# A six-layer mixture-of-experts and attention kernel on one core: expert gates from TensorE, two weight loads from ScalarE, and a transposed output projection

## The reference, cut to what matters

```python
x = x + 0.5 * _L0_ffn_ref(_layernorm(x), Wr, br, W1, b1, W2, b2)    # MOE0_A
x = x + _L0_attn_ref(_layernorm(x), wq, bq, wk, bk, wv, bv, wo, bo) # ATT0
x = x + 0.5 * _L0_ffn_ref(_layernorm(x), Wr, br, W1, b1, W2, b2)    # MOE0_B
x = x + 0.5 * _L1_ffn_ref(_layernorm(x), gate_w, expert_w, expert_b)  # MOE1_A
x = x + _L1_attn_ref(_layernorm(x), Wq, Wk, Wv, Wo)                 # ATT1
x = x + 0.5 * _L1_ffn_ref(_layernorm(x), gate_w, expert_w, expert_b)  # MOE1_B
```

```python
h = gelu(einsum('td,edh->teh', xt, W1) + b1)
o = einsum('teh,eho->teo', h, W2) + b2
y = einsum('teo,te->to', o, comb)
```

```python
V = Q * KV[:, None, :] * Z
out = V @ wo + bo
return gelu(out, approximate=True)
```

## Time and profile before

| | us |
|---|---|
| Median of 3 runs | 703.26 |
| Lowest and highest | 699.38, 709.02 |
| The profiled execution | 708.19 |
| Its span in the profile | 706.2 |
| TensorE busy in the span | 655.9 (93%) |
| VectorE, ScalarE, GpSimd busy | 465.5, 432.3, 181.3 |

### The profile page before, as it was taken

One profiled execution on the slowest core, in us unless ns is written; L12 is line 12 of the kernel. 1 busy time (PEld: TensorE's weight loads), 2 busy tenths in 40 slices (PEclk: granted clock), 3 DMA queues, 4 the chain that ended last, 5 costly groups with the idle time before them and its releaser, 6 DMA issues.

```text
span 706.2 us, 7645 instructions
## 1 busy us (share of the span) xinstructions
PE 655.9 (93%) x2395; PEld 415.2 (59%) x2395; DVE 465.5 (66%) x1059; ACT 432.3 (61%) x922; POOL 181.3 (26%) x132
## 2 busy tenths in 40 slices
PE   3699998999999999999999999999999989889974
PEld 2456565556656555676576666666566645556552
DVE  5677467643447964737769957858886757386752
ACT  4345456444447554697486478657379524968685
POOL 3120000100002111144042025214014432676565
PEclk9899999999999999999999999989999998989998
DMA  8782621063333107612223222200613000000000
GB/s 244 162 164 67 112 63 38 22 122 65 102 75 60 59 3 132 96 26 65 42 61 62 65 55 60 60 1 11 111 60 61 0 1 0 1 15 1 16 16 15
DMA packets 27026, 42.22 MB, mean 60 GB/s; under 512 B 1689, under 2 KB 8938, under 8 KB 26986
## 3 DMA queue, kind: packets, MB, share of 16 engines
q1 hardware_dynamic: 26986, 41.74, 27.1%
HBM read 40.42 MB, written 1.31 MB: 59 GB/s over the span
## 4 chain that ended last, share of the span: by engine, by line
PE 67%; ACT 12%; DVE 9%; SPq 5%; DMA 4%; issue 2%; POOL 1%; POOLq 0%; ACTq 0%; DVEq 0%
PE py L1122 26%; PE ph L900 7%; PE ph L902 7%; PE ph L901 7%; ACT stage L547 5%; ACT bc L547 4%; DMA bc<-comb_rows 3%; PE ps L1030 2%; SPq L358 2%; DVE stage L756 2%; PE ps L1031 2%; PE ps L1032 2%; SPq L331 1%; PE ps L1004 1%; PE ps L1005 1%
## 5 line engine op out<-in xcount | busy, mean ns | idle before, releaser
L596 ACT ACTIVATE g<-ph,b1col 128x512 f32<-128x512 f32 x256 | 172.7, 695 | 153.3 <-PE ph L902 120.1
L1122 PE MATMUL py<-hw,w2s 128*128 128x512 f32 x512 | 250.0, 612 | 1.9 <-DVE hw L859 1.9
L859 DVE TENSOR_TENSOR hw<-g,bc 128x1024 f32<-128x1024 f32 x128 | 166.8, 1310 | 110.4 <-ACT g L596 93.2
L1122 PEld LDWEIGHTS py<-hw,w2s 128*128 128x128 f32 x512 | 97.2, 194 | 77.7 <-issue 64.4
L900 PE MATMUL ph<-xbh,w1h 128*128 128x512 f32 x256 | 137.4, 537 | 0.0
L388 POOL TENSOR_TENSOR rstd<-vare,mhalf 128x4 f32<-128x4 f32 x24 | 35.4, 1477 | 358.3 <-DVE vare L672 358.1
L547 ACT ACTIVATE stage<-ps,comb 128x128 f32<-128x128 f32 x384 | 106.3, 564 | 10.4 <-PE ps L1032 10.2
L902 PE MATMUL ph<-xbh,w1l 128*128 128x512 f32 x256 | 102.7, 401 | 0.0
L901 PE MATMUL ph<-xbl,w1h 128*128 128x512 f32 x256 | 102.6, 401 | 0.0
L448 POOL TENSOR_TENSOR stage<-stage 128x1024 f32<-128x1024 f32 x24 | 57.4, 2393 | 68.4 <-ACT stage L547 68.4
L900 PEld LDWEIGHTS ph<-xbh,w1h 128*128 128x128 f32 x256 | 49.7, 194 | 30.8 <-issue 22.6
(11 more groups left out here) (199 smaller groups left out, 865.0 us busy)
## 6 DMA issues: line engine op xcount, KB each, us to landing
bc<-comb_rows SPq DMA_DIRECT2D x31, 1024.0 KB, 8.8
stage<-in_L_ffn_W_dram SPq DMA_DIRECT2D x4, 512.0 KB, 6.5
X<-in_L_attn_x_dram SPq DMA_DIRECT2D x4, 256.0 KB, 3.1
bc<-comb_rows SPq DMA_DIRECT2D x4, 256.0 KB, 5.5
out_dram<-X SPq DMA_DIRECT2D x4, 256.0 KB, 2.3
comb_rows<-combT SPq DMA_DIRECT2D x8, 32.0 KB, 5.3
side<-in_L_attn_wq_dram SPq DMA_DIRECT2D x1, 64.0 KB
side<-in_L_attn_wk_dram SPq DMA_DIRECT2D x1, 64.0 KB
```

The source lines that it names most:

```text
L596: nc.scalar.activation(g[:, s % 2, h, 0:w], ph[:, (HC * s + h) % RING_PH, 0:w], ACT.Gelu, bias=b1col[:, HC * e + h:HC * e + h + 1]).then_i ...
L859: V.tensor_tensor(hw[:, s % RING_HW, :, 0:w], g[:, s % 2, :, 0:w], bc[:, s // GQ % 2, s % GQ, 0:w].unsqueeze(1).to_broadcast([P, HC, w]), ...
L1122: ins = T.matmul(py[:, 0:cols], w2s[:, w], hw[:, s2 % RING_HW, h, 0:cols], start=e2 == 0 and h == 0, stop=False)
```

## The change

Four parts.

1. **Gates of the first three experts from TensorE.** `PE_GATES` is 3. After `combT` is there, TensorE multiplies it by a column of the identity spread over 128 columns, which gives the row of one expert on all partitions, in one bank of `ps` for each expert. VectorE reads the gates of slots 0 to 2 from there. SyncE reads back only the fourth expert's row for the first group.
2. **Two large loads issued by ScalarE.** W2 is issued after ScalarE's first part of W1 (L484 of the changed kernel), the expert weights of the second kind in its step `wt` (L513), which waits for all parts of `w1_ready`. The attention's and the other small loads stay with SyncE.
3. **Output projection of the first attention.** `wos` is now the stationary operand and all 512 tokens stream past it in one matmul; the result is features by tokens, so the bias is one value for each partition and goes into ScalarE's gelu. TensorE then transposes four tiles into `ps`, and VectorE adds from PSUM. On TensorE the step has one more turn. The bias matmuls and `bos` are gone.
4. **The table of turns** is another one for every engine but SyncE; its first rows show the form:

```diff
-    "PE": ("h5 l3 m2 l m3 l3 m3 l m3 l m2 h m l2 m3 h3 m l h m19 l h2 m5 l m2 h2 m7 h m5 l m2 l2 m2 l m9 l m32 l m4 l m2 h2 m2 l "
+    "PE": ("h4 l3 m4 l m h l m2 l2 m3 l m l m l2 m h m l3 m l3 h3 m h m2 h2 m15 l m4 l m2 h2 m6 h m h m4 l m2 l2 m2 l m11 l m32 l m4 "
```

The rest of the diff:

```diff
@@ -64,6 +64,7 @@
     LAG = 2
+    PE_GATES = 3
@@ -89,9 +90,8 @@
         wr0 = sb("wr0", [P, 2 * E], f32r)
         wr1 = sb("wr1", [P, 2 * E], f32r)
         qkv0h, qkv0l = sb("qkv0h", [P, 3 * P], f32r), sb("qkv0l", [P, 3 * P], f32r)
-        bqkv = sb("bqkv", [P, 3])
+        bqkv = sb("bqkv", [P, 4])
         wos = sb("wos", [P, D])
-        bos = sb("bos", [1, D])
         qkv1h, qkv1l = sb("qkv1h", [P, 3 * P], f32r), sb("qkv1l", [P, 3 * P], f32r)
         woT = sb("woT", [P, P])
         weh, wel = sb("weh", [P, E * D], f32r), sb("wel", [P, E * D], f32r)
@@ -196,12 +196,13 @@
         y_out = sem("y_out")
         comb_row = sem("comb_row")
         bc_in = [sem("bc_in0"), sem("bc_in1")]
-        bc_first = [sem(f"bc_first{e}") for e in range(GQ)]
+        gate_ps = sem("gate_ps")
+        bc_first = sem("bc_first")
 
         light = {n: sem(n) for n in ("stat", "rstd", "xn", "xt_ps", "xh", "xl", "res", "lg_ps", "shift", "expd",
                                   "comb", "ct_ps", "ct", "yt_ps")}
         a0 = {n: sem("a0_" + n) for n in ("q_ps", "k_ps", "v_ps", "relq", "relk", "v", "minq", "mink", "expq", "expk",
-                                          "vz", "o_ps", "o", "x")}
+                                          "vz", "o_ps", "o", "ot_ps", "x")}
         f1 = {(l, late): {n: sem(f"f{l}_{late}_{n}") for n in ("y_ps", "relu_a", "relu_v", "half", "quarter", "sum", "red")}
               for l in (MOE1_A, MOE1_B) for late in (0, 1)}
         a1 = {late: {n: sem(f"a1_{late}_{n}") for n in ("qk_ps", "v_ps", "relu", "v", "exp", "qk", "x", "kv", "kvh", "kvl",
@@ -327,13 +328,12 @@
                 sp.dma_start(stage[:, w1_part(i)].rearrange("p (e h) -> p e h", h=H), W1[e].rearrange("e d h -> d e h")).then_inc(w1_in[i], 16)
                 if i == 0:
                     sp.dma_start(b1row[:, :], b1.rearrange("e (c p) -> (e c) p", p=P)).then_inc(w_in["b1"], 16)
-            sp.dma_start(w2s[:, :].rearrange("p (e c o) -> p e c o", e=E, c=HC), W2.rearrange("e (c p) o -> p e c o", p=P)).then_inc(w_in["w2"], 16)
             sp.dma_start(b2s[:, :], b2).then_inc(w_in["w2"], 16)
             for i, (w, b) in enumerate(((wq, bq), (wk, bk), (wv, bv))):
                 sp.dma_start(stage2[:, E + P * i:E + P * (i + 1)], w).then_inc(w_in["small"], 16)
                 sp.dma_start(bqkv[:, i:i + 1], b.rearrange("(p a) -> p a", a=1)).then_inc(w_in["small"], 16)
             sp.dma_start(wos[:, :], wo).then_inc(w_in["small"], 16)
-            sp.dma_start(bos[:, :], bo.rearrange("(a p) -> a p", a=1)).then_inc(w_in["small"], 16)
+            sp.dma_start(bqkv[:, 3:4], bo.rearrange("(p a) -> p a", a=1)).then_inc(w_in["small"], 16)
             for c in range(1, NCH):
                 sp.dma_start(X[:, col(c)].rearrange("p (t d) -> p t d", d=D), x_t[:, tiles(c), :]).then_inc(x_in[c], 16)
 
@@ -347,13 +347,11 @@
                     if k >= 2:
                         sp.wait_ge(hw_ready, GQ * (k - 1))
                     if k == 0:
-                        for e in range(GQ):
-                            sp.dma_start(bc[:, 0, e:e + 1, 0:wide(c)], comb_dram[l // 2, e:e + 1, col(c)].partition_broadcast(P)).then_inc(bc_first[e], 16)
+                        sp.dma_start(bc[:, 0, PE_GATES:GQ, 0:wide(c)], comb_dram[l // 2, PE_GATES:GQ, col(c)].partition_broadcast(P)).then_inc(bc_first, 16)
                         continue
                     sp.dma_start(bc[:, k % 2, :, 0:wide(c)], comb_dram[l // 2, q * GQ:(q + 1) * GQ, col(c)].partition_broadcast(P)).then_inc(bc_in[k % 2], 16)
                     if k == 1:
                         sp.wait_ge(w1_ready, W1_PARTS)
-                        sp.dma_start(stage[:, 0:E * D].rearrange("p (e h) -> p e h", e=E), expert_w.rearrange("e d h -> d e h")).then_inc(w_in["we"], 16)
                         for i, w in enumerate((Wq, Wk, Wv, Wo)):
                             sp.dma_start(stage[:, E * D + P * i:E * D + P * (i + 1)], w).then_inc(w_in["l1"], 16)
                         sp.dma_start(stage[0:E, E * D + 4 * P:E * D + 5 * P], gate_w).then_inc(w_in["l1"], 16)
@@ -482,6 +480,8 @@
                 for i in range(W1_PARTS):
                     act.wait_ge(w1_in[i], 16)
                     nc.scalar.activation(w1h[:, w1_part(i)], stage[:, w1_part(i)], ACT.Copy).then_inc(w1_high, 1)
+                    if i == 0:
+                        act.dma_start(w2s[:, :].rearrange("p (e c o) -> p e c o", e=E, c=HC), W2.rearrange("e (c p) o -> p e c o", p=P)).then_inc(w_in["w2"], 16)
                     yield
 
             def q0(l, c):
@@ -509,6 +509,8 @@
                 yield
 
             def wt(l, c):
+                act.wait_ge(w1_ready, W1_PARTS)
+                act.dma_start(stage[:, 0:E * D].rearrange("p (e h) -> p e h", e=E), expert_w.rearrange("e d h -> d e h")).then_inc(w_in["we"], 16)
                 for _ in range(WROUNDS + 1):
                     yield
 
@@ -525,7 +527,7 @@
                     nc.scalar.activation(t_m[:, i, :], t_m[:, i, :], ACT.Exp).then_inc(a0["exp" + n], 1)
                 yield
                 act.wait_ge(a0["o_ps"], c + 1)
-                nc.scalar.activation(osb, ps[:, 1, :], ACT.Gelu_apprx_tanh).then_inc(a0["o"], 1)
+                nc.scalar.activation(osb, ps[:, 1, :], ACT.Gelu_apprx_tanh, bias=bqkv[:, 3:4]).then_inc(a0["o"], 1)
                 yield
 
             def f1_(l, c):
@@ -759,8 +761,8 @@
                     ins = V.scalar_tensor_tensor(vv[:, q], t_m[:, 0, q], kvs[:, 1, s:s + 1], t_r[:, 0, q], ALU.mult, ALU.mult)
                 ins.then_inc(a0["vz"], 1)
                 yield
-                dve.wait_ge(a0["o"], c + 1)
-                V.tensor_tensor(X[:, col(c)], X[:, col(c)], osb, ALU.add).then_inc(a0["x"], 1)
+                dve.wait_ge(a0["ot_ps"], c + 1)
+                V.tensor_tensor(X[:, col(c)], ps[:, 2, :], X[:, col(c)], ALU.add).then_inc(a0["x"], 1)
                 yield
 
             def f1_(l, c):
@@ -849,15 +851,17 @@
             def main(s, half):
                 if half and s < SLOTS:
                     dve.wait_ge(g_ready, HC * (s + 1))
-                    if s < GQ:
-                        dve.wait_ge(bc_first[s], 16)
+                    if s < PE_GATES:
+                        dve.wait_ge(gate_ps, s + 1)
+                    elif s == PE_GATES:
+                        dve.wait_ge(bc_first, 16)
                     elif s % GQ == 0:
                         dve.wait_ge(bc_in[s // GQ % 2], 16 * ((s // GQ + 1) // 2))
                     if s >= RING_HW:
                         dve.wait_ge(slot_done, s - RING_HW + 1)
                     w = wide(MAIN[s // E][1])
-                    V.tensor_tensor(hw[:, s % RING_HW, :, 0:w], g[:, s % 2, :, 0:w],
-                                    bc[:, s // GQ % 2, s % GQ, 0:w].unsqueeze(1).to_broadcast([P, HC, w]), ALU.mult).then_inc(hw_ready, 1)
+                    gates = ps[:, s, 0:w] if s < PE_GATES else bc[:, s // GQ % 2, s % GQ, 0:w]
+                    V.tensor_tensor(hw[:, s % RING_HW, :, 0:w], g[:, s % 2, :, 0:w], gates.unsqueeze(1).to_broadcast([P, HC, w]), ALU.mult).then_inc(hw_ready, 1)
 
             def wt(l, c):
 
@@ -910,6 +914,10 @@
                     yield
 
             def q0(l, c):
+                l, c = MAIN[0]
+                pe.wait_ge(light["ct"], nth_light("ct", l, c))
+                for e in range(PE_GATES):
+                    T.matmul(ps[:, e, 0:wide(c)], ident[0:E, e:e + 1].to_broadcast([E, P]), combT[:, col(c)], start=True, stop=True).then_inc(gate_ps, 1)
                 yield
 
             def light_bank(stage_):
@@ -999,11 +1007,12 @@
                 yield
                 yield
                 pe.wait_ge(a0["vz"], c + 1)
+                T.matmul(ps[:, 1, :], wos[:, :], vv, start=True, stop=True).then_inc(a0["o_ps"], 1)
+                yield
+                pe.wait_ge(a0["o"], c + 1)
                 for j in range(TPC):
-                    d = ps[:, 1, j * D:(j + 1) * D]
-                    T.matmul(d, vv[:, j * P:(j + 1) * P], wos[:, :], start=True, stop=False)
-                    ins = T.matmul(d, ones[0:1, :], bos[:, :], start=False, stop=True)
-                ins.then_inc(a0["o_ps"], 1)
+                    ins = T.transpose(ps[:, 2, j * P:(j + 1) * P], osb[:, j * P:(j + 1) * P], ident[:, :])
+                ins.then_inc(a0["ot_ps"], 1)
                 yield
 
             def f1_(l, c):
@@ -1126,6 +1135,7 @@
 
             def wt(l, c):
                 pe.wait_ge(w_in["l1"], 16 * 6)
+                pe.wait_ge(hw_ready, PE_GATES)
                 T.transpose(ps[:, 2, 0:E], be_raw, ident[0:E, 0:E]).then_inc(be_ps, 1)
                 yield
                 pe.wait_ge(we_ready, 1)
```

## The result

The changed kernel takes 698.73 us (median of 20 runs, 697.44 to 703.92), the kernel before 706.21 us in the same comparison (20 runs, 699.38 to 710.43). The ratio is 0.9922, 95% interval 0.9900 to 0.9943. It is faster by 0.8%, which counts as no change by the 2% bound, where 3.4% was predicted: 682, range 670 to 696. The profiled execution of after took 697.63 us.

A forecast was written before the change was run, and what follows sets the result against it. TensorE's own work was taken to bound the main stream, and ScalarE to carry most of the tail. 708.2 - 5.7 (start) - 8.1 (projection) - 7.7 (clock) - 4 (tail) = 682.7, stated as 682, range 670 to 696.

The forecast's parts named there:

- Start, 5.7 predicted: Start: first product with W2 at 25.5 instead of 31.18 us, with ScalarE's second large issue blocked until 19; 5.7 us gained.
- ahead of its use by three slots now: Start: chunk 1's layer norm, which needs its x, was said to come three slots before its result is used.
- the start gives nothing: Rival, start: W2's packets delay W1's last parts, and ScalarE's gelu waits; 688.4, up to 693 us; chance 0.12.
- the move of the loads does nothing: Rival, start: the wait belongs to the shared engines, so SyncE's later loads stay held; about 684 us; chance 0.1.
- Projection, 8.1: First attention's output projections: 2.0 us less TensorE work for each of four chunks, 8.1 us gained.
- clock, 7.7: Behind the four projections: three of four falls of TensorE's clock vanish with the narrow matmuls; 7.7 of 10.3 us gained.
- the clock falls nevertheless: Rival, projections: TensorE still waits for VectorE ahead of them, so the clock still falls; 690.4 us; chance 0.2.
- The cover of the new wait: Projection: a product with W2 (1.72 us) hides TensorE's wait for the gelu; uncovered it costs 0.9 us per chunk.
- I take 4 us of that: Tail behind the main stream, 135.6 us before, at least 116: 4 us gained, bounds -6 to +10.
- by the same step durations the new order gives about 16: Tail: ScalarE's first small activations come about 16 us after the last bias matmul, instead of 19.
- now stand further ahead between the `f1` tiles: Tail: the late chunk's attention steps come earlier, which was to shrink ScalarE's 6.20 us wait ahead of 661.66.
- The slower rival: Rival, tail: GpSimd's chunk 2 outer products queue with halving sums, tail grows by up to 16; about 720 us; chance 0.04.

The follow-up runs named there:

- e6: The kernel before with the first three experts' gates from TensorE and the changed order up to slot 12, loads still issued by SyncE: ratio 0.9978.
- e12: The kernel before with the new output projection, in the changed order from slot 14 to slot 112: 692.88 us, ratio 0.9822.
- e9: The changed kernel with chunk 2's last layer norm step and router moved ahead of the late chunk's attention on VectorE, TensorE and ScalarE: 700.34 us, ratio 0.9919.
- e11: The changed kernel with the second half of the tail (behind chunk 2's second attention and the late chunk's first expert layer) in the old order: 694.37 us, ratio 0.9821.
- e3: The kernel before with the new output projection alone, in the order of the kernel before: 698.75 us, ratio 0.9931.
- e1: The changed kernel with all four engines in the order of the kernel before from slot 112 on: 688.39 us, ratio 0.9782.
- e2: The kernel before with all four engines in the order of the changed kernel from slot 112 on: 716.74 us, ratio 1.0168.
- e4: The changed kernel with the old output projection (eight narrow matmuls per chunk, bias on TensorE), otherwise in the changed order: 715.06 us, ratio 1.0178.
- e5: The changed kernel with the first half of the tail, from slot 112 through chunk 0's last-expert-layer f1, in the old order: 701.17 us, ratio 0.9961.

## Why the prediction was wrong, by its own steps

- **Start, 5.7 predicted, 4.9 measured.** The size was nearly right, and that was luck: a delay that was predicted didn't come, and one that wasn't predicted took its place. ScalarE's issue was to be blocked until 19; it took 0.70, and ScalarE was idle 0.49 ahead of slot 1's gelu, not 1 to 3. What held the product was `x` of chunk 1, which the chain of the prediction didn't have: I had the gated result start as soon as the gate is there, though on VectorE the first steps of that layer norm stand ahead of it; of this norm I only asked when its own result is needed ("ahead of its use by three slots now"). Of SyncE's issues in the first 20 us one took longer than 2: the third load of `x`, 3.11 of the 5.06 for the three. The rival "the start gives nothing" is out: the fourth part of W1 was split from 12.21 us on, and slot 0's gelu started at 16.05, 0.6 sooner than before. So is "the move of the loads does nothing": without it the first product came 1.7 us later (e6).
- **Projection, 8.1, and clock, 7.7: 15.8 predicted, 15.4 measured,** 16.1 in e12. The sum came out, its terms less well. In the main stream of before 12.0 us of clock are lost and in that of after 2.9, so the clock is worth 9.1 (8.5 at the projections, 0.6 at the start) and the work about 6.3. A step takes 1.49 us on TensorE (1.14 from the wide matmul to the next start, 0.35 for the transposes) where 1.31 was said, which makes 7.4 for four; and TensorE now waits 0.78 us for the sum into `X` ahead of the second attention's products (L1056) in chunks 2 and 3, a wait that the prediction didn't have. The full clock behind at least three of four came as said, with some luck: e9 and e11 have the same order there, and two falls each. The rival "the clock falls nevertheless" is out: TensorE waits as long as before or longer (1.93, 1.49, none and 1.50, where before had 1.94, 0.48, 0.61 and 1.47), and the clock stays up in three of four. The rule cited with it, that transposes don't count as busy in the same way (the Trainium skill, TensorE: Matmul & The Clock Gate, Part 4: PE-mode transpose), made no difference that a row here shows: four transposes stand behind each projection of after, with three of four at full clock.
- **The cover of the new wait.** "The new wait, TensorE for the gelu, has a product with W2 (1.72) as cover" held in the changed order and not in the old one (e3: up to 2.94 us). The price given without cover, 0.9 for each chunk, was too low.
- **The failed step is the tail's: "I take 4 us of that".** The term was -4 and measured +9.8; with it right the sum is 696.5. Two steps of its working failed. That "by the same step durations the new order gives about 16" was wrong: the first small activation came after 19.04 us, as before (19.05). In both traces the chain from the last copy of `py` through layer norm and router of chunk 3 leads up to it, and that chain didn't get shorter; e11, with the same order up to there, took 17.7. And the 6.20 us ahead of 661.66 were to shrink because the late attention's steps "now stand further ahead between the `f1` tiles": that is just where it lost. The late attention takes 42.4 us against 34.2 before, and what follows 4.6 more; in the traces steps that were moved ahead stand in line behind others whose inputs aren't ready, on GpSimd, VectorE and TensorE. That the order of this half makes the loss is shown (e11); the single waits are read from the traces.
- **The slower rival had a part of the mechanism,** GpSimd's outer products in line with halving sums that wait for ScalarE. It named chunk 2's attention where it is the late chunk's, and had a chance only as a whole: it was priced for the case that makes the kernel slower (21.5 + 14 us). A tail that grows by about 10 eats half of the gain and needs nothing else to go wrong. The prediction itself had "-6 to +10" for the tail, and 682.7 + 14 = 696.7 lies outside its range.

## What to carry to other kernels

When a change rewrites the table of turns for the whole program, price the order stretch by stretch, apart from the code; a splice of the two tables (here at slot 112) costs one run and told 9.8 us. In a stretch with no engine at full load, an earlier turn is no gain by itself: ask for each moved step what is behind it in line and whether its inputs exist by then. The releaser named at a large wait may be one of several that come almost together. Moving it alone then gives nothing (e9), and that is no proof that it doesn't matter: take the others away with it.

## What was not expected of the hardware

- A multiplication of two SBUF operands on VectorE, 128x512, takes 0.69 us, and 2.03 where it runs into work of GpSimd. After (VectorE, then GpSimd), and e1, where GpSimd is idle:

```profile
646.34 2.03 DVE L839 TENSOR_TENSOR hw<-hw,g 128x512 f32<-128x512 f32 x1
...
645.48 2.34 POOL L446 TENSOR_TENSOR stage<-stage 128x1024 f32<-128x1024 f32 x1 [1.93 <-ACT stage L549]
```

```profile
642.43 0.69 DVE L840 TENSOR_TENSOR hw<-hw,g 128x512 f32<-128x512 f32 x1
```

  It took 2.02 to 2.04 in the five traces with the new order in the second half of the tail (after, e2, e4, e5, e9), and 0.69 in the other nine. The Trainium skill (GPSIMD Engine Reference, Key points) has GpSimd share its SBUF interfaces with VectorE's instructions that have two SBUF inputs; the rows agree. TensorE waits for this instruction (4.39 us, ahead of 648.43), so it is 1.3 of the 8.0 us.
- An issue behind W2 took 9.89 us on SyncE, 10.26 in e6, and 0.75 with W2 on ScalarE's queue; the second large issue on ScalarE took 0.70 at 17.05, while W2 was still under way (issued at 6.19, landed 14.4 later). The wait belongs to what SyncE had already issued, not to the shared engines alone.
- The write of the gates to DRAM was issued at 19.70 and the read that waits for it at 25.68, 6.0 us later, with the expert weights under way; before it was 3.2 (21.44 to 24.65). For the three experts that need it first, it no longer matters.
